# Experts of a decoder: transposed inner values, bias and relu in ScalarE's evacuations, and gates spread by DMA

## The reference

```
x  <- layernorm(x)   (the result is added to the x before)
logits = xf @ Wr + br
_, topk_idx = jax.lax.top_k(logits, 2)
mask  = zeros_like(logits).at[arange(T)[:, None], topk_idx].set(1.0)
gates = mask + logits - stop_gradient(logits)
h = relu(einsum('td,edh->eth', xf, W1) + b1[:, None, :])
combined = einsum('te,eth,ehd->td', gates, h, W2) + gates @ b2
return xf + combined
```

## Time and profile before

| | |
|---|---|
| median of 3 runs | 4094.79 us |
| the profiled execution's own time | 4099.99 us |
| its span | 4098.0 us |
| experts: first instruction to the end of the span | 3740.4 to 4098.0 us |
| busy share of the span: PE, PEld, DVE, ACT, POOL | 94%, 73%, 73%, 69%, 46% |

### The profile page before, as it was taken

One profiled execution on the slowest core, in us unless ns is written; L12 is line 12 of the kernel. 1 busy time (PEld: TensorE's weight loads), 2 busy tenths in 40 slices (PEclk: granted clock), 3 DMA queues, 4 the chain that ended last, 5 costly groups with the idle time before them and its releaser, 6 DMA issues. The chain is left out here.

```text
span 4098.0 us, 106550 instructions
## 1 busy us (share of the span) xinstructions
PE 3856.6 (94%) x33992; PEld 2995.1 (73%) x33992; DVE 3004.8 (73%) x7523; ACT 2829.1 (69%) x6420; POOL 1878.4 (46%) x1792
## 2 busy tenths in 40 slices
PE   7999899999979999898999989999999989998999
PEld 5666688888746666685666677888888867776777
DVE  7888655555569999658999955777777767776665
ACT  5666455555569999757999965777777757775333
POOL 5444322222268888526777753333333321112443
PEclk9999899999999999999999999999999989999999
DMA  0000100000000000100000010000000000000000
GB/s 19 9 9 10 48 8 6 6 6 6 26 25 8 8 8 8 27 17 10 8 8 8 14 27 29 1 0 0 0 0 0 0 3 4 3 3 6 12 12 12
DMA packets 109258, 42.46 MB, mean 10 GB/s; under 512 B 91232, under 2 KB 107872, under 8 KB 108512
## 3 DMA queue, kind: packets, MB, share of 16 engines
q1 hardware_dynamic: 109152, 41.10, 3.9%
HBM read 20.16 MB, written 4.19 MB: 6 GB/s over the span
## 5 line engine op out<-in xcount | busy, mean ns | idle before, releaser
L1152 POOL TENSOR_TENSOR l_rc<-l_rc,l_rs 128x1024 f32<-128x1024 f32 x128 | 303.7, 2373 | 201.5 <-DVE l_rs L1344 201.5
L1219 ACT ACTIVATE l_prob<-l_prob,l_mx 128x128 f32<-128x128 f32 x1024 | 312.0, 389 | 0.0
L1830 POOL TENSOR_TENSOR mb_steps<-w_upto,mb_dta 128x1024 f32<-128x1024 f32 x64 | 121.5, 1898 | 353.7 <-DVE mb_dta L2087 353.7
L721 POOL TENSOR_TENSOR ca_prob<-ca_prob,ca_sm 128x1232 f32<-128x1232 f32 x64 | 144.0, 2250 | 299.3 <-DVE ca_sm L887 299.3
L1244 PE MATMUL l_qk_ps<-w_local,l_hT 128*128 128x512 f32 x512 | 248.9, 609 | 13.4 <-DVE l_rs L1344 11.4
L1146 POOL TENSOR_TENSOR l_prob<-l_prob,l_sm 128x1024 f32<-128x1024 f32 x128 | 243.0, 1899 | 18.4 <-DVE l_sm L1330 18.4
L1129 POOL TENSOR_TENSOR l_rc<-l_rc,l_ss 128x1024 f32<-128x1024 f32 x128 | 243.6, 1903 | 12.5 <-POOL l_rc L1152 4.5
L1987 PE MATMUL mb_x_ps<-w_wx,mb_xT 128*128 128x256 f32 x1024 | 237.2, 385 | 0.0
L2552 POOL TENSOR_TENSOR mo_hid<-mo_hid,mo_gate 128x1024 f32<-128x1024 f32 x64 | 121.8, 1903 | 199.4 <-DVE mo_hid L2698 199.4
L1339 DVE TENSOR_REDUCE l_ss<-l_sq 128x16 f32<-128x1024 f32 x128 | 156.1, 1219 | 77.8 <-ACT l_sq L1183 77.4
L1987 PEld LDWEIGHTS mb_x_ps<-w_wx,mb_xT 128*128 128x128 f32 x1024 | 190.2, 191 | 23.3
(11 more groups left out here) (355 smaller groups left out, 12065.8 us busy)
## 6 DMA issues: line engine op xcount, KB each, us to landing
la_xin<-in_x SPq DMA_DIRECT2D x64, 64.0 KB
l_h<-lt_y SPq DMA_DIRECT2D x128, 32.0 KB
lt_quad<-lt_y SPq DMA_DIRECT2D x32, 128.0 KB
out_x<-k_x SPq DMA_DIRECT2D x64, 64.0 KB, 1.5
l_h<-lt_y SPq DMA_DIRECT2D x128, 31.8 KB
lt_quad<-lt_y SPq DMA_DIRECT2D x32, 127.0 KB
ca_ctxT<-in_ctx_T SPq DMA_DIRECT2D x128, 19.2 KB
wr_state<-in_p_state SPq DMA_DIRECT2D x1, 2438.5 KB, 11.9
```

Source lines behind the costliest of these rows:

```text
L721: gp.tensor_tensor(prob[b.slot][:], prob[b.slot][:], sm[b.lane][:, 1].unsqueeze(2).to_broadcast([T, H, S]), ALU.mult).then_inc(*pool_prob. ...
L1152: gp.tensor_tensor(wide(rc[l][:]), wide(rc[l][:]), wide(rs[l][:]), ALU.add).then_inc(*pool_sum.did("rot"))
L1219: ex = sc.activation(p[:, a, j], p[:, a, j], ACT.Exp, bias=mx[l][:, a, j:j + 1])
```

## The change

The inner values are now computed transposed from the start: `hid_ps[:, l, j]` is one of eight 128 by 128 blocks with the inner values of two experts on the partitions and the tokens along the row, from eight matmuls with W1 as weights (L2641 of the new kernel). ScalarE takes each out of PSUM with b1 as a bias on its partitions and a relu (L2603, eight instructions), into `hidT`, which is four deep. The eight transposes, VectorE's addition of b1 and the tile `hid` are gone.

The gates must now lie along the row, the same for 64 partitions. VectorE writes them in another order (`by_half`, first the even experts and then the odd ones, L2686), TensorE and ScalarE transpose them to 16 by 128 (L2624, L2589). SyncE writes these 8 KB to DRAM (`parked`, L2532), waits for that, and reads them back twice: eight gate rows of 128 tokens (4 KB) for each of 64 partitions, once for the even and once for the odd experts (L2536), 512 KB together, into `spread`. GpSimd multiplies `hidT` by `spread` (L2562). `b2` is laid out in the order of the gates.

`chosen` and its copy are gone: VectorE overwrites the six lesser ones of the eight largest logits in place (a memset, L2675). xn is made last in VectorE's step, after the gates. The pipeline has one stage more: NORM, TURN, ROUTE, GATE, SPREAD, OUT for n to n-5, and its loop covers four steps instead of two.

```diff
-                    b = at(LAST)
+                    b = at(GATE)
+                    if b:
+                        sp.wait_ge(*act_gate.at("gT", b))
+                        sp.dma_start(g.parked[b.lane], gateT[b.slot][:]).then_inc(parked[b.lane], 16)
+                        sp.wait_ge(parked[b.lane], b.loaded())
+                        for a in (0, 1):
+                            src = g.parked[b.lane].rearrange("(a j) t -> a (j t)", a=2)[a].partition_broadcast(64)
+                            sp.dma_start(spread[b.lane][64 * a:64 * a + 64].rearrange("p j t -> p (j t)"), src).then_inc(spread_in[b.lane], 16)
+                    b = at(OUT)
...
-                        gp.wait_ge(*vec_hid.at("hb", b))
-                        gp.tensor_tensor(hid[l][:], hid[l][:], gate[l][:].unsqueeze(2).to_broadcast([T, E, HID]), ALU.mult
+                        hid = hidT[b.slot][:]
+                        gp.wait_ge(*act_hid.at("h1", b))
+                        gp.wait_ge(spread_in[b.lane], b.loaded(32))
+                        gp.tensor_tensor(hid, hid, spread[b.lane][:], ALU.mult).then_inc(*pool_hid.did("hid"))
...
+                    b = at(GATE)
+                    if b:
+                        sc.wait_ge(*pe_gate.at("gT", b))
+                        sc.wait_ge(*pe_out.at("y", b, ago=4))
+                        sc.wait_ge(*pool_hid.at("hid", b, ago=2))
+                        sc.activation(gateT[b.slot][:], gate_ps[0:E, 0:T], ACT.Copy).then_inc(*act_gate.did("gT"))
...
+                            for j in range(4 * u, 4 * u + 4):
+                                ex = sc.activation(hidT[b.slot][:, j], hid_ps[:, b.lane, j], ACT.Relu, bias=b1[:, j:j + 1])
+                            ex.then_inc(*act_hid.did(f"h{u}"))
...
+                    b = at(OUT)
+                    if b:
+                        te.wait_ge(*pool_hid.at("hid", b))
+                        te.wait_ge(*vec_out.at("x", b, ago=1))
+                        for j in range(CH):
+                            te.matmul(y_ps[:, 0:C], hidT[b.slot][:, j], w2[:, j], start=(j == 0), stop=False)
+                        te.matmul(y_ps[:, 0:C], gateT[b.slot][:], b2, start=False, stop=True).then_inc(*pe_out.did("y"))
...
+                        te.wait_ge(*act_hid.at("h1", b, ago=2))
                         for u in (0, 1):
                             for j in range(4 * u, 4 * u + 4):
-                                mm = te.transpose(turn_ps[:, j], hid[l][:, 2 * j:2 * j + 2].rearrange("p e h -> p (e h)"),
-                                                  g.ident[:])
...
+                                mm = te.matmul(hid_ps[:, l, j], w1[:, j], xnT[l][:], start=True, stop=True)
+                            mm.then_inc(*pe_route.did(f"h{u}"))
...
-                        v.tensor_copy(chosen[l][:, 0:K], top[l][:, 0:K]).then_inc(*vec_route.did("chosen"))
-
+                        v.memset(top[l][:, K:8], LOW).then_inc(*vec_route.did("chosen"))
...
-                        v.wait_ge(*vec_route.at("gate", b))
-                        v.wait_ge(*pe_route.at("h", b))
-                        v.wait_ge(*pe_out.at("hT1", b, ago=2))
-                        v.tensor_tensor(hid[l][:].rearrange("p e h -> p (e h)"), hid_ps[:].rearrange("p a n -> p (a n)"), b1,
-                                        ALU.add).then_inc(*vec_hid.did("hb"))
```

More of the change, by code:

```diff
@@ L2486, in experts @@
         part = g.experts_part
-        w1 = part["w1"].rearrange("p (e h) -> p e h", e=E)
+        w1 = part["w1"].rearrange("p (j n) -> p j n", j=CH)
         w2 = part["w2"].rearrange("p (j c) -> p j c", j=CH)
@@ L2492, in experts @@
         stats, mv, rstd = both(m, "stats", [T, 6]), both(m, "mv", [T, 2]), both(m, "rstd", [T, 2])
-        hid = both(m, "hid", [T, E, HID])
         logit, left = both(m, "logit", [T, E + 8]), both(m, "left", [T, E + 8])
-        top, chosen = both(m, "top", [T, 8]), both(m, "chosen", [T, 8])
+        top = both(m, "top", [T, 8])
         carrier = both(m, "carrier", [T, 2])
-        gate = both(m, "gate", [T, E])
-        hidT, gateT = both(m, "hidT", [128, CH, T]), both(m, "gateT", [E, T])
-        hid_ps = m.ps("hid_ps", [128, 2, 512])
+        gate, by_half = both(m, "gate", [T, E]), both(m, "by_half", [T, E])
+        hidT = [m.sb(f"hidT{i}", [128, CH, T]) for i in range(4)]
+        gateT = [m.sb(f"gateT{i}", [E, T]) for i in range(4)]
+        spread = both(m, "spread", [128, CH, T])
+        hid_ps = m.ps("hid_ps", [128, 2, CH, T])
         route_ps = m.ps("route_ps", [128, 512])
         xn_ps = m.ps("xn_ps", [128, 512])
-        turn_ps = m.ps("turn_ps", [128, CH, T])
         gate_ps = m.ps("gate_ps", [128, 512])
@@ L2598, in step @@
                 def step(at):
-                    b = at(OUT)
-                    if b:
-                        l = b.lane
-                        te.wait_ge(*vec_route.at("gate", b))
-                        te.wait_ge(*act_out.at("hT1", b, ago=1))
-                        te.transpose(gate_ps[0:E, 0:T], gate[l][:], g.ident[:]).then_inc(*pe_out.did("gT"))
                     b = at(TURN)
@@ L2609, in step @@
                         te.transpose(xn_ps[:, 0:T], xn[b.lane][:], g.ident[:]).then_inc(*pe_turn.did("xnT"))
+                    b = at(GATE)
+                    if b:
+                        te.wait_ge(*vec_route.at("gate", b))
+                        te.wait_ge(*act_gate.at("gT", b, ago=1))
+                        te.transpose(gate_ps[0:E, 0:T], by_half[b.lane][:], g.ident[:]).then_inc(*pe_gate.did("gT"))
+                    b = at(OUT)
+                    if b:
+                        te.wait_ge(*pool_hid.at("hid", b))
[3 more added lines that the diff above has]
+                        te.matmul(y_ps[:, 0:C], gateT[b.slot][:], b2, start=False, stop=True).then_inc(*pe_out.did("y"))
                     b = at(ROUTE)
@@ L2682, in step @@
                                         ).then_inc(*vec_norm.did("xn"))
[L2683 to L2701 removed]
+                pipeline(v, g.NB, OUT + 1, step, turn=4)
 class Globals:
@@ L2756 @@
     out = nc.dram_tensor("out_x", arrays["x"].shape, F32, kind="ExternalOutput").ap()
+    dram["parked"] = nc.dram_tensor("parked", [2, 16, T], F32, kind="Internal").ap()
     decoder(nc, dram, out)
```

106 lines of the change are left out of this document (41 added, 65 removed).

## The result

| | before | after |
|---|---|---|
| median of 8 runs | 4096.01 us | 4106.93 us |
| lowest to highest | 4093.77 to 4099.92 | 4102.22 to 4108.88 |
| profiled execution, span | 4098.0 | 4100.5 |

The account below looks back on a forecast made before the run. TensorE bounded the experts at 5.43 us a block; afterwards the gates' loop through DRAM would, at 4.96. 63 steps save 29.6 us, the drain costs 4.7, so 4094.8 - 25 = 4070 us, range 4050 to 4094.

Parts of the forecast that it names:

- the drain: End of the experts, last router matmul to last addition: 13.7 us after instead of 9.0, so 4.7 more.
- loop B: Gates' way through DRAM, GpSimd's product, mask, gates and xn back to TensorE: 14.87 us over three periods, 4.96 a step.
- the trip: Gates written to DRAM by SyncE and read back until GpSimd can start: 5.55 us.
- loop A: Over VectorE, from xn's transpose through router, logits, mask and gates to xn, made last: period 4.87 us.
- the two ends: Fill and drain of the experts' pipeline: fill taken as even, drain 4.7 us longer.
- TensorE's list: TensorE's own work per block of 128 tokens: 4.63 us after the change instead of 5.43, 0.80 less.
- the reads run at half the rate: Rival: each read covers only 64 partitions, so reads take 4.9 instead of 3.6 us; 4084 to 4098 us, chance 0.22.
- The estimate that the prediction drew from the Trainium skill: Partitions 0 to 63 reach half the ports: pure transfer 2.4 instead of 1.3 us, kernel 4082 to 4095 us.
- The fill: Start of the experts' pipeline: no change, as first steps lack output matmuls but the first output waits for the DRAM transfers.
- Small steps: Evacuations 0.27 us each, the last 0.37; memset 0.10 to the next instruction; x's store late with no one waiting.
- The slower rival: Gates' reads land so late that the gain is eaten, from 6.9 us for write and reads, period 5.39; chance 0.06.
- three loops: Candidates for the step's period: TensorE's own work 4.63 us, the path over VectorE 4.87, the gates' path through DRAM 4.96.

Follow-up runs that it names:

- e10: Changed kernel with one more step between gates' DMAs and multiply, xn ahead of the mask, gates' transpose behind the output, one woven read: 4045.1 us.
- e1: Changed kernel, but only blocks 0 and 1 send their gates through DRAM, later blocks reuse those buffers: 4089.3 us, step 5.22.
- e4: Changed kernel with one step more between the gates' DMAs and the multiply, and four buffers for the spread gates: 4086.5 us, step 5.20.
- e5: No decoder, only DMA forms and GpSimd products timed alone: two half reads 4.59 us from issue to mark, one read to 128 partitions 3.59.
- e9: Changed kernel with the two halves of a chunk woven, so one DMA fills all 128 partitions instead of two: 4090.7 us, step 5.24.
- e3: Changed kernel with xn made ahead of the mask, behind `match_replace`, instead of after the gates: 4100.5 us, step 5.31.
- e13: Changed kernel with one step more between gates' DMAs and multiply, and xn made ahead of the mask: 4075.3 us, step 4.97.
- e15: Changed kernel with extra matmuls in TensorE's idle time ahead of the last two outputs: 4101.8 us, drain 19.6.

## Why the prediction was wrong

In short: of the 29.6 us that the steps were to give, none came. The steps of the changed kernel, the first eight included, took 2.1 us more than before, and the drain 9.1 more instead of 4.7. Four terms of the sum were too small: in loop B the reads of the trip (3.95 us forecast with issue and handing on, 4.7 in the mean) and the product (1.90, measured 2.35), the floor of loop A (4.87, measured 5.2), and the two ends.

**TensorE's list: right.** 4.63 us was forecast, e10 runs it in 4.53.

**Loop B: the right loop, two terms too small.** From xn's transpose (3894.35) to the one three steps later (3910.55) the forecast path can be followed, and its parts add up:

| us | forecast | measured |
|---|---|---|
| to the end of the gates' copy | 6.48 | 6.55 |
| trip | 5.55 | 6.29 |
| GpSimd's product | 1.90 | 2.35 |
| end of product to next xn transpose | 0.94 | 1.01 |
| a third of the sum | 4.96 | 5.40 |

The mask ends with the product (3909.57 against 3909.54), as forecast, but is held for only 0.04 us there: in this last of the three steps (5.17 us) loops A and B all but tie, and it is the first (5.54) that the product before made longer, by 0.4 us (the mask of 0.58 us). With the mean reads of 4.71 the third of the sum is 5.33. That the wait for the trip costs something beyond loop A is shown by e1 and e4, which take it away and have steps of 5.2. The trip's error lies in the reads, 4.93 here and 4.71 in the mean instead of 3.95; the small write, 1.36 instead of 1.6, gave something back. The rival "the reads run at half the rate" named 4.9 us and comes close by luck: the packets of e5 show no halved rate, but time ahead of the first and behind the last packet and a second issue. The estimate that the prediction drew from the Trainium skill, a trip of 6.1 to 6.6 us, fits the 6.29 in the same way. The forecast had 0.2 us for there being two DMAs; with one in their place (e9) the reads land 0.7 sooner. The product's 0.45 had a row. The page of before shows a GpSimd product of two full operands over 128x1024, at 2373 ns:

```profile
L1152 POOL TENSOR_TENSOR l_rc<-l_rc,l_rs 128x1024 f32<-128x1024 f32 x128 | 303.7, 2373 | 201.5 <-DVE l_rs L1344 201.5
```

I took the duration of the instruction that was removed, of the same size, and not that of one with the same operands.

**Loop A: too small by 0.30 us, and this alone would have spoiled the forecast.** In the step above: turn to router 2.70 (forecast 2.60), router to logits 0.45 (0.40), to the memset 0.44 (0.42), to the match load 0.11 (0.10), to the mask 0.28 (0.29), mask to the last gate 0.45 (0.41), to xn 0.26 (0.18), xn 0.35 (0.35), to TensorE 0.13 (0.12): 5.17 against 4.87. No term is off by more than 0.10; they lean to one side. The 0.10 is the two transposes with nothing running ahead of them (0.33 instead of 0.22), the 0.08 is the distance from the instruction ahead of xn to xn. Behind `match_replace`, where the 0.18 was read, xn comes 0.22 later in e3 and e13, and behind `by_half` 0.26; what makes either longer, no run shows. e1 and e4 show the floor that this makes: 5.2. With it, even a trip of 5.55 and a product of 1.90 would have gained some 63 x 0.23 = 14 us in the steps: 4085 us with the ends as forecast, and about nothing with what the two ends cost.

**The ends: forecast 4.7 us more, measured 13.5.** The fill was taken as even and costs 4.4: the first output waits 4.17 us and then runs at the 1.2 GHz level. Of the drain, to the last addition, 18.1 us were measured for 13.7: the write 2.87 (1.6), since it stood behind the reads of the block before, the reads 4.80 (3.95), the product 2.34 (1.9), and output with b2 3.93 (2.4) at the lower level. e1 puts 7.6 us of the drain on the trip, e15 1.6 on the clock.

**Small steps: right.** Eight evacuations 2.17 us (2.26), the memset 0.11 to the next instruction (0.10), ScalarE and the narrower matmuls nowhere in the way, x's store late (3.5 us to landing instead of 1.5) and nobody waiting for it.

**The slower rival** was set at a trip of 6.9 us; the kernel was slower at 6.29 already, because the product, loop A's floor and both ends took the rest. The chances went wrong there: 0.82 for faster rested on three loops within 0.35 us of each other, each counted with gaps of 0.05 to 0.1, and errors of that kind add up over ten terms.
